# Landing the adjacency of a graph kernel in two halves, and turning both halves of E back to back

## The reference

```
deg  = clip(adj.sum(axis=1), 1);  dis = deg ** -0.5
diffusion = (dis[:,None] * adj * dis[None,:]) @ x - x
sim  = x @ x.T / (|x_i| |x_j|)
attn = softmax(beta * sim * adj, axis=1)
x1   = layernorm(x + diffusion + sigmoid(alpha) * (attn @ x - x))
out  = layernorm(x1 + relu(adj @ (x1 @ weights)))
```

## Time and profile before

| | |
|---|---|
| median of 3 runs | 665.28 us |
| profiled execution: its own time, and its span | 666.4 us, 664.5 us |
| TensorE busy | 639.2 us, 96% of the span |
| VectorE, ScalarE, GpSimd busy | 520.8, 414.0, 258.7 us |
| DMA engines, 100 to 380 us | busy 98 to 101% of the time, 254 to 269 GB/s |
| adjacency load, turn of E, turn of the packed adjacency: median from issue to landing | 4.4, 5.3, 4.6 us |

### The profile page before, as it was taken

How to read it: one execution, slowest core, us unless ns; L and a number is a source line. 1 busy time by engine, 2 the same in 40 slices (tenths; PEclk the granted TensorE clock), 3 DMA queues, 4 the chain that set the end, 5 groups by cost and what they waited for, 6 DMA issues and landing times. The chain is left out here.

```text
span 664.5 us, 16212 instructions
## 1 busy us (share of the span) xinstructions
PE 639.2 (96%) x5079; PEld 464.2 (70%) x5079; DVE 520.8 (78%) x1566; ACT 414.0 (62%) x775; POOL 258.7 (39%) x249
## 2 busy tenths in 40 slices
PE   6779999999999999999999999899999999999996
PEld 6446667777777777777777776798888874444466
DVE  4878889999999899999999999867777772333443
ACT  4998889899999999999999998611111110000000
POOL 2899546556556456456465468400000000000000
PEclk9999999999999999999999999999999999999999
DMA  7599999999999999999999995500000000000000
GB/s 255 168 235 251 250 259 259 255 263 266 259 266 262 276 254 253 267 267 244 283 270 253 258 266 95 99 1 1 0 0 0 0 0 1 16 17 16 16 33 33
DMA packets 165164, 107.43 MB, mean 162 GB/s; under 512 B 144400, under 2 KB 148752, under 8 KB 165136
## 3 DMA queue, kind: packets, MB, share of 16 engines
q1 hardware_dynamic: 164704, 107.04, 61.4%
q10 hardware_dynamic: 432, 0.07, 0.1%
HBM read 69.34 MB, written 2.10 MB: 107 GB/s over the span
## 5 line engine op out<-in xcount | busy, mean ns | idle before, releaser
L985 PE MATMUL ps_s<-xn_parts,xn_signed 128*128 128x512 f16 x756 | 203.7, 379 | 5.6 <-DVE cmax L714 5.6
L714 DVE CUSTOM_DVE_ANT_1 scores<-ps_s,adj_bytes 128x512 f32<-128x512 f32 x252 | 171.4, 682 | 20.6 <-PE ps_s L985 14.2
L530 ACT ACTIVATE scores<-scores,col 128x1024 f32<-128x1024 f32 x128 | 157.4, 1232 | 3.1 <-DVE col L725 2.9
L476 ACT ACTIVATE adj_bytes<-land 128x1024 uint8<-128x1024 f32 x128 | 133.5, 1047 | 2.5 <-POOL packed L339 2.2
L347 POOL TENSOR_SCALAR e_parts<-scores 128x1024 f16<-128x1024 f32 x64 | 71.9, 1124 | 139.5 <-ACT scores L530 86.9
L1114 PE MATMUL ps_e<-y_parts,stage 128*128 128x256 f16 x896 | 98.0, 273 | 0.0
L985 PEld LDWEIGHTS ps_s<-xn_parts,xn_signed 128*128 128x128 f16 x756 | 68.2, 98 | 42.0 <-DVE cmax L714 5.7
L1114 PEld LDWEIGHTS ps_e<-y_parts,stage 128*128 128x128 fp8e4 x896 | 87.7, 98 | 10.1
L735 DVE SCALAR_TENSOR_TENSOR e_parts<-scores,e_parts 128x1024 f16<-128x1024 f32 x64 | 92.6, 1447 | 2.7 <-POOL e_parts L347 2.7
L537 ACT ACTIVATE eT_parts<-ps_e 128x512 f16<-128x512 f32 x128 | 75.9, 593 | 24.2 <-PE ps_e L996 23.5
L729 DVE SCALAR_TENSOR_TENSOR eT_parts<-ps_e,eT_parts 128x512 f16<-128x512 f32 x128 | 87.5, 684 | 1.5 <-ACT eT_parts L537 1.5
(11 more groups left out here) (129 smaller groups left out, 990.9 us busy)
## 6 DMA issues: line engine op xcount, KB each, us to landing
land<-in_adj SPq DMA_DIRECT2D x128, 512.0 KB, 4.4
x_keep<-in_x SPq DMA_DIRECT2D x4, 512.0 KB, 9.5
out<-u SPq DMA_DIRECT2D x7, 256.0 KB, 2.1
eTx<-e_parts SPq DMA_TRANSPOSE x64, 5.3
packT<-packed SPq DMA_TRANSPOSE x16, 4.6
out<-u SPq DMA_DIRECT2D x2, 128.0 KB, 1.7
eT_parts<-in_L_gnn_weights ACTq DMA_DIRECT2D x1, 64.0 KB, 8.9
scores<-in_L_gnn_weights SPq DMA_DIRECT2D x1, 64.0 KB, 1.9
```

Of the source, the lines that this page charges most:

```text
L476: nc.scalar.activation(adj_bytes[:, q, i * CH:(i + 1) * CH], land[:, i, :], ACT.Copy, scale=float(BYTE_TOP[q] >> i), accum_out=deg[:, i, b ...
L530: nc.scalar.activation(piece, piece, ACT.Exp, bias=neg_max[q], scale=abs_beta, accum_out=csum[:, q, i:i + 1]).then_inc(exp_done, 1)
L714: nc.vector.tensor_tensor_reduce(scores[:, q, o:o + BANK].rearrange("p (k q) -> p k q", k=K), score_bank(h, r == 0 if start else False).re ...
L985: ins = nc.tensor.matmul(score_bank(h, start), xn_signed[:, q, part, :], xn_parts[:, other, o:o + BANK], start=(part == 0 and other == 0), ...
```

## The change

`land` gets a second half: row block r now lands in half r mod 2, each half with its own four semaphores. A load therefore waits for the cast of the row block two before it, and the eight loads of row blocks 0 and 1 wait for nothing. In the loop, the four loads of row block b*4+k are issued together; behind them, for even k, one `turn_adj`; then both pieces of E of row block b*4+k-3, one after the other. So SyncE's order for one body becomes: piece 0 of E(r), piece 1 of E(r), loads 0 to 3 of r+4, every second body `turn_adj`, piece 0 of E(r+1). The first `turn_adj` now stands ahead of piece 0 of E(1). Behind the loop `turn_adj(14)` comes first, then both pieces of row blocks 29, 30 and 31, then `turn_adj(15)`. ScalarE's casts read the half of their row block. Nothing else of the other engines' work is changed, and the number of DMAs and of bytes stays the same.

```diff
--- before.py
+++ after.py
@@ -84,7 +84,7 @@
 
         packT = sb("packT", [P, R // 2 * W], U32)
         stage = sb("stage", [P, G, C * W], U32)
-        land = sb("land", [P, C, CH], F32)
+        land = sb("land", [P, 2, C, CH], F32)
         x_keep = sb("x_keep", [P, R, D], F32)
         adj_bytes = sb("adj_bytes", [P, 2, N], U8)
         x_parts = sb("x_parts", [P, R, 2 * D], F16)
@@ -133,7 +133,7 @@
         small_loaded = sem("small_loaded")
         eps_set = sem("eps_set")
         w_loaded = sem("w_loaded")
-        land_full = [sem(f"land_full{i}") for i in range(C)]
+        land_full = [[sem(f"land_full{q}_{i}") for i in range(C)] for q in range(2)]
         ident_zero = sem("ident_zero")
         ident_done = sem("ident_done")
         squares_done = sem("squares_done")
@@ -221,7 +221,7 @@
         var = [mv[:, n, 1:2] for n in range(G)]
         words = [adj_bytes[:, q, :].bitcast(U32).rearrange("p (i w) -> p i w", i=C) for q in range(2)]
         packed_half = [packed[:, m, :].bitcast(U16) for m in range(2)]
-        stages = [land[:, :, :].bitcast(U32), stage[:, :, :]]
+        stages = [land[:, 0, :, :].bitcast(U32), stage[:, :, :]]
         quads8 = [a.bitcast(F8).rearrange("p n (b i k) -> p b k n i", b=B, k=K) for a in stages]
         stage8 = [stage[:, n, :].bitcast(F8).rearrange("p (b i k) -> p b i k", b=B, k=K) for n in range(G)]
 
@@ -238,7 +238,8 @@
 
             def land_piece(b, k, i):
 
-                sp.dma_start(land[:, i, :], adj_v[b, k // K, k % K, :, i * CH:(i + 1) * CH]).then_inc(land_full[i], 16)
+                sp.dma_start(land[:, k % 2, i, :],
+                             adj_v[b, k // K, k % K, :, i * CH:(i + 1) * CH]).then_inc(land_full[k % 2][i], 16)
 
             def turn_adj(m, q):
 
@@ -253,36 +254,28 @@
                                        e_parts[:, n, :, :].rearrange("p a j -> p (a j)")).wait_op(
                                            x_loaded[0], 16, "sem-ge").then_inc(ex_turned[n], 16)
 
-            for i in range(C):
-                land_piece(0, 0, i)
-            for k in range(1, G):
+            for k in range(G):
                 for i in range(C):
-                    sp.wait_ge(cast_done, (k - 1) * C + i + 1)
+                    if k >= 2:
+                        sp.wait_ge(cast_done, (k - 2) * C + i + 1)
                     land_piece(0, k, i)
-                    if k == G - 1 and i == 1:
-                        turn_ex(0, 0, 1)
-                if k == G - 2:
-                    turn_ex(0, 0, 0)
-                if k == G - 1:
-                    turn_ex(1, 1, 0)
-            turn_adj(0, 0)
+                    if k == G - 1 and i == 2:
+                        turn_ex(0, 0, 0)
+            turn_ex(0, 0, 1)
             with sp.Fori(1, Q) as b:
                 for k in range(G):
-                    r, q = b * G + (k - 3), (k + 1) % 2
+                    r, q = b * G + (k - G), k % 2
                     for i in range(C):
-                        sp.wait_ge(cast_done, b * (G * C) + ((k - 1) * C + i + 1))
+                        sp.wait_ge(cast_done, b * (G * C) + ((k - 2) * C + i + 1))
                         land_piece(b, k, i)
-                        if i == 1:
-                            turn_ex(r, q, 1)
-                    if k == 1:
-                        turn_adj(b * 2 + (-1), 1)
-                    if k == 3:
-                        turn_adj(b * 2, 0)
+                    if q == 0:
+                        turn_adj(b * 2 + (k // 2 - 2), k // 2)
                     turn_ex(r + 1, 1 - q, 0)
+                    turn_ex(r + 1, 1 - q, 1)
+            turn_adj(R // 2 - 2, 0)
             for r in (R - 3, R - 2, R - 1):
+                turn_ex(r, r % 2, 0)
                 turn_ex(r, r % 2, 1)
-                if r < R - 1:
-                    turn_ex(r + 1, (r + 1) % 2, 0)
             turn_adj(R // 2 - 1, 1)
             sp.wait_ge(e_turned, R * TB)
             sp.wait_ge(ex_lo, 2 * R)
@@ -472,8 +465,8 @@
 
                 if not first:
                     act.wait_ge(packed_done, r - 1)
-                act.wait_ge(land_full[i], r * 16 + 16)
-                nc.scalar.activation(adj_bytes[:, q, i * CH:(i + 1) * CH], land[:, i, :], ACT.Copy,
+                act.wait_ge(land_full[q][i], r * 8 + (16 - 8 * q))
+                nc.scalar.activation(adj_bytes[:, q, i * CH:(i + 1) * CH], land[:, q, i, :], ACT.Copy,
                                      scale=float(BYTE_TOP[q] >> i), accum_out=deg[:, i, bass.ds(r, 1)]).then_inc(cast_done, 1)
```

## The result

The changed kernel takes 667.60 us (median of 13 runs, 666.55 to 669.41), the kernel before 665.69 (13 runs): ratio 1.0032, interval 1.0024 to 1.0041. It is slower by 1.9 us or 0.3%, where a gain of 0.7 us (664.6) was forecast; the time lies inside the stated range (663.2 to 668.8).

A forecast was written before the change was run, and what follows sets the result against it. TensorE, issuing without a gap in the steady bodies, was taken as the bound, leaving only early stalls to win. Terms 0 + 0 + 1.8 - 0.5 - 2.36 + 0.3 = -0.7 took 665.28 to 664.6 us; range 663.2 to 668.8.

The forecast's parts named there:

- Piece 0 of E(0) earlier: Prologue: the turn goes out at about 35.9, the 2.16 us stall goes, all given back by body 2; value 0.
- The first `turn_adj` ahead of piece 0 of E(1): Body 1: piece 0 of E(1) lands at 58.15 instead of 56.34; cost +1.8 us, bounds +1.5 and +3.0.
- What the later stalls give back: Bodies 2 to 5: stalls of 0.50 and 2.36 us go, body 5 begins at 99.9; bounds -2.0 and +1.3.
- I am wrong if ... body 5 begins more than 1.3 us away from 100.91: Failure signs: body 5 that far off, or pitch above 12.3 with TensorE waits on `eTx` in many bodies.
- Loads two row blocks ahead: Prologue: the eight loads no longer wait, a 0.20 us cast wait goes; value 0, bounds -0.2 and +1.
- The steady bodies: Bodies 5 to 29: four loads right ahead of piece 0 add +0.3 us over all bodies.
- GpSimd's wait for turns: Sign: this wait shrinks from 39 us by half or more, and that changes nothing.
- piece 0 is late in every body: Rival, steady bodies: turns exceed the slack of 0.1 to 0.7 us, lengthening bodies; 669 as a whole; chance 0.17.
- the loss at body 1 is not given back: Rival, bodies 1 to 5: the turn takes 5.7 us and later stalls move along, near +1.7, 667.0; chance 0.10.

The follow-up runs named there:

- e5: The changed kernel run again, unchanged, on another chip: 667.46 us, ratio to before 1.0028.
- e7: The changed kernel with 13 extra products of the identity on TensorE in its two waits of body 1: 666.20 us, ratio to before 1.0014.
- e2: The kernel before with only the first `turn_adj` put ahead of piece 0 of E(1): 666.30 us, ratio to before 1.0020.
- e9: The kernel before, run again unchanged with its own profile: 665.61 us, ratio to before 1.0007.
- e3: The kernel before with two landing halves and loads two row blocks ahead, turns in the order of before: 664.91 us, ratio to before 0.9993.
- e8: The kernel before with piece 0 of E(0) turned one load earlier and the first `turn_adj` ahead of piece 0 of E(1): 666.23 us, ratio 1.0006.
- e1: The changed kernel with the first `turn_adj` moved behind piece 0 of E(1): 664.92 us, ratio to before 0.9994.
- e11: e3 with piece 0 of E(0) turned early and the first `turn_adj` ahead of piece 0 of E(1): 666.93 us, ratio to before 1.0022.
- e10: e1 with GpSimd's signed block of row block 3 ahead of its high part of piece 1 of E(1): 665.12 us, ratio to before 1.0000.
- e6: The changed kernel with piece 0 of E(0) turned late, behind all loads of row block 3: 666.27 us, ratio to before 1.0010.
- e13: e11 with the first `turn_adj` behind piece 0 of E(1) and 5 extra products before TensorE's signed-block wait in body 1: 664.42 us, ratio to before 0.9981.
- e12: e1 with 5 extra products on TensorE ahead of its wait for GpSimd's signed block in body 1: 664.63 us, ratio to before 0.9989.
- e15: The kernel before with 6 extra products on TensorE ahead of its wait for piece 0 of E(0) in body 0: 664.49 us, ratio 0.9987.

## Why the forecast was wrong

Counted from body 0 to body 5 the forecast is 65.5 us (34.41 to 99.9), the profile has 67.37. Of these 1.9 us, 0.3 lie ahead of the first use of E(1) and 1.6 behind it: from there to body 2 the forecast has 5.05 us (58.15 to 63.2), measured are 6.64 (57.68 to 64.32). The rest of the miss is in the profile that the forecast started from.

**"Piece 0 of E(0) earlier ... Value 0, bounds -0.3 and 0."** This is the step that failed. The turn went out at 35.10 and the stall at 43.84 went, and the gain was given back in body 1 as written. What I had not priced is that idle time is not neutral by where it lies. TensorE came to body 1 1.4 us sooner, counted from body 0 (13.06 us instead of 14.42), waited for GpSimd, and ran into the wait for E(1) behind it: 3.4 us idle within 4.2. The kernel before had 1.47 and 1.67 us of waits in body 0, within 5.8 us, and next to none in body 1. The clock fell in body 1 of the changed kernel, and stayed up in the kernel before. That costs 1.3 us in the median (e5 against e7), 1.7 in the profile. The term had no entry for the clock: its value and its upper bound were both 0, as if it made no difference where the idle time lies.

**"The first `turn_adj` ahead of piece 0 of E(1) ... Cost +1.8."** The mechanism and the place were right: the issue at 53.23 (53.65 forecast), landing at 57.6 (58.15). One reading behind it was wrong: the 4.3 us of the earlier trace rows were taken for a turn with no loads ahead, but SyncE's queue has two loads at 196.74 and a `turn_adj` at 197.94 ahead of that turn. In the changed kernel the turns of E between 100 and 380 us, with four loads ahead, took 4.3 us in the median, against 5.1 before; the four loads did not add to that median. Alone the late turn makes +0.65 us (e2), as the later stalls take part of it back.

**"What the later stalls give back."** Bodies 2 to 5 took 36.70 us, forecast 36.7. But the 2.36 us were those of one execution; e9 had 1.37 (38.06 less three bodies of 12.23). Summing on one profile and applying the difference to the median took about 1 us too much. Together: 1.3 for the clock and 1.0 for the profile are 2.3 of the 2.6 us that the forecast is off (1.9 against -0.7). The sum as written, 1.8 - 0.5 - 2.36 + 0.3, is -0.76, so it should have read -0.8.

**"I am wrong if ... body 5 begins more than 1.3 us away from 100.91."** It began at 101.02, and the pitch was 12.24, so neither sign fired although the forecast failed. In this profile body 0 began 0.76 us earlier than in the first, and the first profile was itself 0.9 us slower than e9 from body 0 to body 5 (66.50 against 65.60). Against e9 the changed kernel is 1.8 us longer there (67.37), e5 1.9 (67.50), which is the measured loss.

**"Loads two row blocks ahead ... Value 0."** Right for ScalarE's wait (0.2 us), and e3 shows no cost. Missed was that with E(0) turned early, only loads two ahead keep a cast of row block 2 from waiting behind that turn (e8): they are part of what makes TensorE early.

**"The steady bodies ... +0.3."** Right in size: 0.1 us in the changed kernel's profile, up to 1.2 in others with that order (e1). GpSimd's wait for turns went from 39.0 us to

```profile
POOL e_parts L340 <- DMA eTx<-e_parts: 0.2, 1, 0.2
```

and nobody gained by it, as the forecast said. The rival "piece 0 is late in every body" did not come. The rival "the loss at body 1 is not given back", 667.0, had nearly the measured time and the wrong reason: the stalls did close.

## What to carry to other kernels

Before counting a removed wait as free gain or as harmlessly given back, add up the idle time of TensorE that ends in one place: two waits close behind each other can cost its clock. Here 1.36 and 2.02 us with 0.8 us of products between did, and so did the like pairs of e5 and e11; one wait of 1.85 (e2) or 1.94 us (e10) did not; but e6 shows that waits 2.6 us apart are no safe case. When a new order makes an engine early, look at what is then issued ahead of the transfer that it will wait for; here moving one small DMA behind another took back 2.5 us. And take a second profile of the kernel before: a stall that stands in one execution may not be there to be won.

## What the runs showed that was not expected

A fall of the clock in the middle of a kernel whose TensorE is busy 96% of the time, after 3.4 us of idle in two parts; and that, to go by the mean clocks, it is not the same in every execution. The runs of the changed kernel go from 0.988 to 0.995 in mean clock and from 666.55 to 669.41 us; the kernels with products in the waits have means of 0.9948 (e7, e13) and 0.9954 (e12), but e15 has 0.9943. The profiled execution of the changed kernel has 0.994 and one fall; the median of its runs is at 0.991, 2 us of full clock less over 665 us (an estimate), so many executions may lose it more than once, or for longer in the prologue. Which is not shown, as each kernel has one profile. The mean clock does not order the kernels by itself: e8 has 0.9948 and is 0.6 us slower than before.
